# Key and value projections of a cross attention as seven block products each, on one core

## The chip, the cores and the metric

The kernel runs on one core of one Trainium2 chip. The metric is the device time of one execution in microseconds (us). Everything is in float32, and so is every product on the tensor engine. The trace holds two records for each such product (one product of a 128x128 weight block with 512 columns is two records), so a count in the profile is twice the count in the code.

## The reference, cut to what matters

The network has two layers on 32 sequences of 32 positions and width 512: gated attention to a context, self attention, a mixture of 32 experts, and then a second layer, which opens with the cross attention that the change concerns:

```python
q = _split_heads(x1 @ Wq.T + bq, HEADS)        # x1: 32 x 32 x 512
k = _split_heads(x2 @ Wk.T + bk, HEADS)        # x2: 32 x 257 x 512, the context
v = _split_heads(x2 @ Wv.T + bv, HEADS)
scores = jnp.einsum('bhqd,bhkd->bhqk', q, k) / jnp.sqrt(jnp.float32(dh))
attn = jax.nn.softmax(scores, axis=-1)
out = jnp.einsum('bhqk,bhkd->bhqd', attn, v)
```

Each of the 32 sequences has its own 257 context rows, so keys and values are 32 products of 257x512 by 512x512 each. After it come a gated decay attention with group norms, a feed-forward part of width 1024, and one 512x512 product for the spectral mix.

## The kernel before, in words

Rows are worked on in 8 tiles of 128 (four sequences each). After the experts, the last stage runs, tile by tile, three generators on each engine: `head(i)` (layer norm, transposition, queries), `cross(i)` (attention to the context, four context blocks, one for each sequence) and `tail(i)` (everything after it), with `ended(i)` for the spectral mix. A hand-written string, `PLAN_C`, sets the order in which they advance, a piece at a time: c for `cross`, t for `tail`, h for `head`, p for `ended`. Each engine walks the same string, so on each engine the pieces stand in the same order, and the engine does them strictly in that order. Engines wait for each other by counting semaphores.

`cross` has seven pieces for each block, here c0 to c6, and `tail` has fifteen for each tile, t0 to t14. With them the string for a tile is

```
block 0: c0 p t0 | c1 c2 c3 t1 | c4 c5 t2 | c6
block 1: c0 t3 | c1 c2 t4 h0 | c3 c4 t5 h1 | c5 t6 h2 | c6
block 2: c0 t7 | c1 c2 c3 t8 | c4 c5 t9 | c6
block 3: c0 t10 | c1 t11 | c2 c3 t12 | c4 t13 | c5 c6 t14
```

The first tile has `PLAN_F` (no tail; DVE adds expert results and GpSimd issues the gathers for them in its t places), the last `PLAN_Y` (no head).

On the tensor engine (PE) a block before the change is: c0 scores (L1711); c1 and c2 one half of the values each (`values`, L1696, four products of 512 columns); c3 the transposition of the normalised weights (L1726); c4 and c5 the keys of the next block (`keys`, L1679, sixteen products of 257 columns); c6 weights times values (L1752). The scalar engine (ACT) does the exponentials (L890) in c0, copies the transposed weights (L897) in c3, and moves the keys out of PSUM with their bias (`keys_out`, L877) in c4 and c5. The vector engine (DVE) takes maxima and normalises in c0 (L1308 to L1314) and moves the values out with their bias (`values_out`, L1299) in c1 and c2. It does nothing in c4 to c6. GpSimd (POOL) does nothing in `cross`; in the tail it computes the power -1/2 for the norms (L576).

The tail's pieces that matter here: t0 output product (PE) and on DVE layer norm and group sums (L1345 to L1270); t1 a small product of group sums (PE, L1768) and on DVE `group_norm` (L1272, with a power on POOL inside it); t2 transpositions; t3 the qkv product, which ACT squares, copies and scales (L918 to L922); t5 scores of the decay attention, on DVE `decayed` (L1338); t6 its product with the values, which waits for `decayed`; t7 and t8 repeat t0 and t1 in form; t9 two additions on DVE (L1368, L1369); t10 to t13 the feed-forward part; in t13 DVE adds its result and does a layer norm (L1375 to L987). h0 is a layer norm on DVE, h2 the query product.

```python
def values(n, s):
    group(ps[:, bV(n), :],
          [(ctxT_c[:, k, s * S + n * P:s * S + (n + 1) * P], WvT_sb[:, k, :]) for k in range(KD)], v_ps)

def group_norm(w, src, at, bank):
    dve.wait_ge(w.gst_ps, at)
    ...
    TS(gvar, gvar, 0.0, GN_EPS, ALU.max, ALU.add).then_inc(w.gv_rdy, 1)
    ...
    dve.wait_ge(w.grs_rdy, at)
```

The opening of the stage, between the last expert and the first scores, computes keys and values of block 0 and the value row of the 257th context row of all sequences (`lasts`, L1845), while GpSimd gathers the expert results of tile 0 (L650), which DVE adds (`add_experts`, L1259) before the first layer norm.

## Time and profile before

| | us |
|---|---|
| median of 3 runs | 1935.95 (1934.34 to 1938.89) |
| the profiled execution, its own time | 1926.86 |
| its span | 1925.2 |
| PE busy in it | 1844.9 (96%) |
| DVE, ACT, POOL busy | 713.3 (37%), 549.1 (29%), 188.1 (10%) |
| granted TensorE clock, mean | 0.977 of full speed |

The rows are read so: a row of a timeline gives the start in us from the start of the span, the length, the engine, the line of the code, the operation with its operand shapes, and how many instructions are merged in it; in square brackets stands how long the engine had been idle and on whom it had waited. Products overlap: the length of one is longer than the step to the next, so steps are taken from starts. A product group that is written through the helper `group` shows the helper's line, L1416.

### The profile page before, as it was taken

What the parts mean: (1) busy time and instruction counts of PE and PEld (TensorE: products, weight loads), DVE (VectorE), ACT (ScalarE), POOL (GpSimd) and SP (SyncE); (2) the same over time, 40 slices, a digit from 0 to 9 for tenths busy, and PEclk for the clock granted to TensorE, in tenths of its full rate; (3) what the DMA queues carried; (4) which work ended last, traced back from release to release, by engine and by line L of the source; (5) the groups of instructions that cost most, each with busy time, mean ns of one, the idle gap of its engine ahead of it and who ended that gap; (6) DMA issues with size and microseconds to landing.
All of it is one profiled execution on the core that took longest, in us unless ns stands there. A gap on an engine that the chain in (4) does not pass through costs nothing.

```text
span 1925.2 us, 35009 instructions
## 1 busy us (share of the span) xinstructions
PE 1844.9 (96%) x15118; PEld 917.9 (48%) x15118; DVE 713.3 (37%) x1541; ACT 549.1 (29%) x1178; POOL 188.1 (10%) x156
## 2 busy tenths in 40 slices
PE   5999879999999999999989999999999999999977
PEld 2454553333333233223346566665656566565644
DVE  3777753222222222222224443333334333434422
ACT  1444302222222222222222232333323233232321
POOL 2222240000000000000011100001000000100000
PEclk9999879999999999999999999999999999999988
DMA  9754377999999999999962300001000100100000
GB/s 362 236 187 172 141 298 301 402 404 405 404 409 408 408 406 409 409 408 404 366 229 78 121 23 27 14 23 28 23 18 23 29 12 24 28 23 18 12 1 11
DMA packets 84703, 370.67 MB, mean 193 GB/s; under 512 B 7407, under 2 KB 25327, under 8 KB 51841
## 3 DMA queue, kind: packets, MB, share of 16 engines
q1 hardware_dynamic: 79744, 355.78, 48.1%
q0 software_dynamic: 4864, 13.51, 2.0%
q8 instruction: 74, 1.21, 0.3%
q14 instruction: 21, 0.16, 0.0%
HBM read 353.14 MB, written 16.84 MB: 192 GB/s over the span
## 4 chain that ended last, share of the span: by engine, by line
PE 89%; DVE 3%; issue 3%; ACT 3%; DMA 1%; POOL 1%; POOLq 0%; DVEq 0%; ACTq 0%
PE ps L1416 41%; PE ps L1600 17%; PE ps L1612 17%; PE ps L1831 3%; PE ps L1726 1%; PE ps L1480 1%; ACT arena L723 1%; PE ps L1752 1%; PE ps L1588 1%; PE ps L1464 1%; PE ps L1711 1%; PE ps L1426 1%; PE ps L1801 0%; POOL arena L576 0%; PE ps L1809 0%
## 5 line engine op out<-in xcount | busy, mean ns | idle before, releaser
L1416 PE MATMUL ps<-arena 128*128 128x512 f32 (+3 forms) x3120 | 886.3, 440 | 18.4 <-ACT arena L723 6.5
L1416 PEld LDWEIGHTS ps<-arena 128*128 128x128 f32 x3120 | 526.8, 193 | 345.0 <-issue 278.5
L1612 PE MATMUL ps<-arena 128*32 128x512 f32 x2304 | 341.9, 593 | 0.0
L1614 PE MATMUL ps<-arena 128*32 128x512 f32 x768 | 340.9, 593 | 0.0
L1600 PE MATMUL ps<-arena 128*32 128x512 f32 x3072 | 339.5, 596 | 0.2 <-issue 0.2
L576 POOL TENSOR_TENSOR arena<-arena 128x1 f32<-128x1 f32 (+3 forms) x80 | 134.6, 1683 | 974.0 <-DVE arena L982 499.6
L1600 PEld LDWEIGHTS ps<-arena 128*32 128x32 f32 x3072 | 98.1, 108 | 235.2 <-issue 233.7
L1612 PEld LDWEIGHTS ps<-arena 128*32 128x32 f32 x2304 | 92.7, 109 | 215.5 <-issue 212.9
L1218 DVE STREAM_TRANSPOSE arena<-arena 128x512 f32<-128x512 f32 x96 | 68.4, 713 | 215.9 <-ACT arena L831 215.9
L831 ACT ACTIVATE arena<-ps 128x512 f32<-128x512 f32 x96 | 57.3, 597 | 276.4 <-PE ps L1600 276.4
L1228 DVE TENSOR_TENSOR arena<-ps,arena 80x512 f32<-80x512 f32 x32 | 22.0, 688 | 306.8 <-ACT arena L844 306.8
L844 ACT ACTIVATE arena<-ps 32x512 f32<-32x512 f32 x96 | 56.7, 591 | 228.4 <-PE ps L1614 228.4
L880 ACT ACTIVATE arena<-ps,arena 128x257 f32<-128x257 f32 x128 | 60.6, 475 | 186.9 <-PE ps L1416 186.9
L1301 DVE TENSOR_TENSOR arena<-ps,arena 128x512 f32<-128x512 f32 x64 | 44.1, 690 | 124.5 <-PE ps L1416 124.0
L897 ACT ACTIVATE arena<-ps 128x512 f32<-128x512 f32 x64 | 34.8, 595 | 185.3 <-PE ps L1726 185.2
L1308 DVE TENSOR_REDUCE arena<-ps 128x1 f32<-128x257 f32 x128 | 53.5, 418 | 85.8 <-PE ps L1711 85.8
L640 POOL DMA_DIRECT2D y_rows<-arena x32 | 16.6, 517 | 676.7 <-DVE arena L1228 676.7
L1614 PEld LDWEIGHTS ps<-arena 128*32 128x32 f32 x768 | 81.5, 109 | 0.0
L890 ACT ACTIVATE arena<-ps,arena 128x257 f32<-128x257 f32 x128 | 60.5, 475 | 53.4 <-DVE arena L1309 53.3
L1221 DVE TENSOR_TENSOR arena<-arena 128x512 f32<-128x512 f32 x96 | 66.5, 693 | 7.1 <-DVE arena L1218 4.8
L1831 PE MATMUL ps<-arena 128*128 128x512 f32 x128 | 60.9, 621 | 0.0
L838 ACT ACTIVATE arena<-arena 128x512 f32<-128x512 f32 x96 | 53.1, 620 | 0.0
(200 smaller groups left out, 1249.1 us busy)
## 6 DMA issues: line engine op xcount, KB each, us to landing
arena<-in_w SPq DMA_DIRECT2D x64, 4096.0 KB, 18.5
arena<-in_ctxT SPq DMA_DIRECT2D x8, 2056.0 KB, 7.8
arena<-in_ctxT SPq DMA_DIRECT2D x32, 514.0 KB, 3.8
arena<-in_ctx SPq DMA_DIRECT2D x8, 2048.0 KB
xe_rows<-arena SPq DMA_DIRECT2D x8, 640.0 KB, 14.3
y_rows<-arena POOLq DMA_DIRECT2D x32, 160.0 KB, 6.4
arena<-xe_rows SPq DMA_DIRECT2D x30, 160.0 KB, 18.8
arena<-in_wqkv0T SPq DMA_DIRECT2D x1, 3072.0 KB, 19.6
```

Of the source, the lines that this page charges most:

```text
L576: pool.tensor_tensor(dst, src, half_sb[:, 0:src.shape[-1]], ALU.pow).then_inc(done, 1)
L831: act.activation(h_sb[:, t, :].rearrange("p (a c f) -> p a c f", a=HB, c=HB), ps[:, t, :].rearrange("p (a f c) -> p a c f", a=HB, c=HB), A ...
L844: act.activation(yq_sb[s][q4[t], :], ps[q4[3], bQ(s, t), :], ACT.Copy).then_inc(yp_out, 1)
L880: act.activation(kT_c[:, m, :], ps[:, bK(m), 0:S], ACT.Identity, bias=bk_sb[:, m:m + 1], scale=1.0).then_inc(k_ev, 1)
L890: act.activation(P_c[:, g, 0:S], ps[:, bS(g), 0:S], ACT.Exp, bias=nmx[:, g:g + 1], scale=SCALE, accum_out=smc[:, g:g + 1]).then_inc(exp_c, 1)
L1218: dve.transpose(hT[s][:, t].rearrange("p n u -> p (n u)"), h_sb[:, t, :]).then_inc(hT_raw, 1)
L1221: TT(h4, h4, bc(b.rearrange("p c n -> p n c").unsqueeze(3), P, HB, HB, T), ALU.add).then_inc(hb_rdy, 1)
L1416: ins = pe.matmul(dst, lhsT, rhs, start=(n == 0), stop=(n == len(pairs) - 1))
L1600: ins = pe.matmul(ps[q4[n], t, :], xeT[s][:, k, q4[t]], w1_c[:, k, n], start=(k == 0), stop=(k == KD - 1))
L1612: pe.matmul(ps[q4[g], bY(s), :], hT[s][:, g, t, q4[c]], w2_sb[s][:, t * HB + c, :], start=(t == 0 and c == 0), stop=(t == ST - 1 and c == ...
L1614: ins = pe.matmul(ps[q4[ST], bQ(s, t), :], hT[s][:, t, ST, q4[c]], w2_sb[s][:, ST * HB + c, :], start=(c == 0), stop=(c == HB - 1))
L1831: ins = pe.matmul(ps[:, w.b7, :], w.hT2[:, f, :], fw2_sb[:, f, :], start=(f == 0), stop=(f == FT2 - 1))
```

## The change

A block's keys and values (256 of its 257 rows) are computed by the seven-product scheme of Strassen in Winograd's form. The 512x512 weight and the context block are cut into four quarters each; instead of eight block products, seven products of sums of quarters are formed. For the keys a block product is four matrix instructions of 128 columns (`key_product`), for the values two of 256 columns (`value_product`). The sums of weight quarters are formed once, on DVE (`weight_sums`); the four sums of context quarters (T1 to T4) are formed for each block on GpSimd, in c2 and c3 of the block before. The results of the products are combined as they are moved out of PSUM: ACT copies the first product (with the key bias), DVE adds the others, seven additions for the values (c1 to c3) and eight, and a small copy, for the keys (c4 to c6). Three PSUM banks are used in turn, so a product waits until the one that had its bank has been read: the fourth for ACT, the fifth, sixth and seventh for DVE's additions. The keys of the 257th row of all sequences are computed once in the opening (`lasts`), where the values' row was already. The value bias goes in through the accumulation of the weighted values. Keys, values and weights of the first block are set up in the opening, on DVE in a new order. Plans, tails and heads are untouched.

On PE the seven products of the values are spread as v1 to v4 in c1, v5 and half the transpositions in c2, v6, v7 and the other half in c3; the keys as k1 to k4 in c4, k5 and half of the weighted values in c5, k6, k7 and the other half in c6.

```diff
+        NP = 7
+        K_ACT, K_DVE, V_DVE = KH, 9, 7
+        N_T = 4
...
+        kX, kY, kZ = 3, 0, 2
+        vX, vY, vZ = 0, 1, 2
+        def bT(j): return (3, 1)[j]
...
+                    if following:
+                        pool.wait_ge(ctxc_in[(bb + 1) % 2], 16 * ((bb + 1) // 2 + 1))
+                        pool.wait_ge(v_ps, NP * bb + 3)
+                        pool.tensor_tensor(T1, B12, B11, ALU.subtract).then_inc(T_rdy, 1)
+                        pool.wait_ge(T_rdy, N_T * (bb + 1) + 1)
+                        pool.tensor_tensor(T2, B22, T1, ALU.subtract).then_inc(T_rdy, 1)
+                        pool.tensor_tensor(B12, B22, B12, ALU.subtract).then_inc(T_rdy, 1)
+                    yield
+                    if following:
+                        pool.wait_ge(v_ps, NP * bb + 6)
+                        pool.wait_ge(T_rdy, N_T * (bb + 1) + 2)
+                        pool.tensor_tensor(T4, B21, T2, ALU.subtract).then_inc(T_rdy, 1)
+                    yield
...
+            def keys_first(bb):
+                act.wait_ge(k_ps, NP * bb + 1)
+                for m in range(KH):
+                    act.activation(kC11[:, m, :], ps[:, kX, m * P:(m + 1) * P], ACT.Identity,
+                                   bias=bk_sb[:, m:m + 1], scale=1.0).then_inc(k_act, 1)
+
+            def values_first(bb):
+                act.wait_ge(v_ps, NP * bb + 1)
+                act.activation(vC11, ps[:, vX, 0:HF], ACT.Copy).then_inc(v_act, 1)
...
+            def weight_sums(A11, A12, S1, A22, S2, S3, S4):
+                TT(S3, A11, S1, ALU.subtract).then_inc(S_rdy, 1)
+                step(TT(S1, S1, A22, ALU.add))
+                step(TT(S2, S1, A11, ALU.subtract))
+                TT(S4, A12, S2, ALU.subtract).then_inc(S_rdy, 1)
...
+            def keys_first(bb):
+                dve.wait_ge(k_act, K_ACT * bb + KH)
+                dve.wait_ge(k_ps, NP * bb + 2)
+                TT(kC12, half(kY), kC11, ALU.add).then_inc(k_dve, 1)
+                dve.wait_ge(k_ps, NP * bb + 4)
+                TT(kC11, half(kX), kC11, ALU.add).then_inc(k_dve, 1)
+
+            def keys_second(bb):
+                dve.wait_ge(k_ps, NP * bb + 5)
+                dve.wait_ge(k_dve, K_DVE * bb + 1)
+                for m in range(KH):
+                    STT(kC21[:, m, :], ps[:, kY, m * P:(m + 1) * P], dbk[:, m:m + 1], kC12[:, m, :],
+                        ALU.add, ALU.add).then_inc(k_dve, 1)
+                dve.wait_ge(k_dve, K_DVE * bb + 4)
+                TT(kC22, half(kZ), kC21, ALU.add).then_inc(k_dve, 1)
+                TT(kC12, half(kZ), kC12, ALU.add).then_inc(k_dve, 1)
+
+            def keys_third(bb):
+                dve.wait_ge(k_ps, NP * bb + 6)
+                TT(kC21, half(kX), kC21, ALU.add).then_inc(k_dve, 1)
+                dve.tensor_copy(kT_c[:, :, 2 * P:S], klast[:, :, bb:bb + 1]).then_inc(k_dve, 1)
+                dve.wait_ge(k_ps, NP * bb + 7)
+                dve.wait_ge(k_dve, K_DVE * bb + 6)
+                TT(kC12, half(kZ), kC12, ALU.add).then_inc(k_dve, 1)
+
+            def values_first(bb):
+                dve.wait_ge(v_act, bb + 1)
+                dve.wait_ge(v_ps, NP * bb + 2)
+                TT(vC12, ps[:, vY, 0:HF], vC11, ALU.add).then_inc(v_dve, 1)
+                dve.wait_ge(v_ps, NP * bb + 4)
+                TT(vC11, ps[:, vX, 0:HF], vC11, ALU.add).then_inc(v_dve, 1)
+
+            def values_second(bb):
+                dve.wait_ge(v_ps, NP * bb + 5)
+                dve.wait_ge(v_dve, V_DVE * bb + 1)
+                TT(vC21, ps[:, vY, 0:HF], vC12, ALU.add).then_inc(v_dve, 1)
+                dve.wait_ge(v_dve, V_DVE * bb + 3)
+                TT(vC22, ps[:, vZ, 0:HF], vC21, ALU.add).then_inc(v_dve, 1)
+                TT(vC12, ps[:, vZ, 0:HF], vC12, ALU.add).then_inc(v_dve, 1)
+
+            def values_third(bb):
+                dve.wait_ge(v_ps, NP * bb + 6)
+                TT(vC21, ps[:, vX, 0:HF], vC21, ALU.add).then_inc(v_dve, 1)
+                dve.wait_ge(v_ps, NP * bb + 7)
+                dve.wait_ge(v_dve, V_DVE * bb + 5)
+                TT(vC12, ps[:, vZ, 0:HF], vC12, ALU.add).then_inc(v_dve, 1)
...
+            keys_first(0)
+            weight_sums(A11v, A12v, S1v, A22v, S2v, S3v, S4v)
+            keys_second(0)
+            dve.wait_ge(lasts_ps, 2)
...
+            keys_third(0)
+            dve.wait_ge(lasts_ps, 3)
+            dve.tensor_copy(vlast_all[0:B, :], ps[0:B, 7, :]).then_inc(lasts_dve, 1)
+            for stage in (values_first, values_second, values_third):
+                stage(0)
+            step(dve.memset(one.PTd, 0.0))
             dve.wait_ge(gathered0, 32)
             add_experts(0)
...
+            def key_product(bank, Sb, Tb):
+                for m in range(KH):
+                    group(ps[:, bank, chunk(m)], [(Sb[:, k, chunk(m)], Tb[:, k, :]) for k in range(KH)],
+                          k_ps if m == KH - 1 else None)
+
+            def value_product(bank, Tb, Sb):
+                group(ps[:, bank, 0:HF], [(Tb[:, k, :], Sb[:, k, :]) for k in range(KH)], v_ps)
+
+            def keys_first(bb):
+                B11, T3, B21, B22 = keys_of(bb % 2)
+                pe.wait_ge(ctxc_in[bb % 2], 16 * (bb // 2 + 1))
+                if bb > 0:
+                    pe.wait_ge(pt_ev, 2 * (bb - 1) + 1)
+                    if bb % NB == 0:
+                        pe.wait_ge(lastX_rdy, bb // NB)
+                key_product(kX, A11k, B11)
+                if bb > 0:
+                    pe.wait_ge(v_dve, V_DVE * (bb - 1) + 6)
+                pe.wait_ge(T_rdy, N_T * bb + 3)
+                key_product(kY, S2k, T2)
+                if bb > 0:
+                    pe.wait_ge(v_dve, V_DVE * bb)
+                key_product(kZ, S1k, T1)
+                pe.wait_ge(k_act, K_ACT * bb + KH)
+                key_product(kX, A12k, B21)
...
+            def keys_second(bb):
+                B11, T3, B21, B22 = keys_of(bb % 2)
+                pe.wait_ge(k_dve, K_DVE * bb + 1)
+                key_product(kY, S3k, T3)
...
+                B11, T3, B21, B22 = keys_of(bb % 2)
+                pe.wait_ge(T_rdy, N_T * bb + N_T)
+                pe.wait_ge(k_dve, K_DVE * bb + 2)
+                key_product(kX, A22k, T4)
+                pe.wait_ge(k_dve, K_DVE * bb + 6)
+                key_product(kZ, S4k, B22)
...
+            def values_first(bb):
+                B11, T3, B21, B22 = keys_of(bb % 2)
+                if bb > 0:
...
+                value_product(vX, B11, A11v)
...
+                value_product(vY, T2, S2v)
...
+                value_product(vZ, T1, S1v)
+                pe.wait_ge(v_act, bb + 1)
+                value_product(vX, B21, A12v)
+
+            def values_second(bb):
+                B11, T3, B21, B22 = keys_of(bb % 2)
+                pe.wait_ge(v_dve, V_DVE * bb + 1)
+                value_product(vY, T3, S3v)
+
+            def values_third(bb):
+                B11, T3, B21, B22 = keys_of(bb % 2)
+                pe.wait_ge(v_dve, V_DVE * bb + 2)
+                value_product(vX, T4, A22v)
+                pe.wait_ge(v_dve, V_DVE * bb + 5)
+                value_product(vZ, B22, S4v)
...
+                    for half in range(2):
+                        if following:
+                            (keys_second, keys_third)[half](bb + 1)
+                        if half == 0:
+                            pe.wait_ge(pt_ev, 2 * bb + 2)
+                            pe.wait_ge(v_dve, V_DVE * bb + V_DVE)
+                            if b == 0:
+                                pe.wait_ge(vlast_in, 16 * HQ * (i + 1))
+                        for g in range(2 * half, 2 * half + 2):
+                            if g == HG - 1 and following:
+                                pe.wait_ge(k_dve, K_DVE * bb + 2 * K_DVE)
...
+                for m in range(KD):
+                    lo = [(A11k, clastT[:, 0:KH]), (A12k, clastT[:, KH:KD])]
+                    hi = [(S1k, clastT[:, 0:KH]), (A22k, dT)]
+                    group(ps[:, 5, (KD + m) * B:(KD + m + 1) * B],
+                          [(w[:, k, chunk(m % KH)], c[:, k, :]) for w, c in (hi if m >= KH else lo) for k in range(KH)],
+                          lasts_ps if m == KD - 1 else None)
...
+            lasts_turned()
+            keys_first(0)
+            keys_second(0)
+            keys_third(0)
...
+            pe.wait_ge(S_rdy, 4)
             lasts()
+            values_first(0)
+            values_second(0)
+            values_third(0)
```

Where it moves instructions, in three places. First DVE, block 0 of a middle tile, from the group sums of t0 to the next maxima; before (L1268 to L1270 are t0, L1301 the values, L1274 to L1281 `group_norm` in t1):

```order
L1268 TENSOR_TENSOR arena<-arena 128x512
L1269 TENSOR_REDUCE arena<-arena 128x16
L1270 TENSOR_REDUCE arena<-arena 128x16
L1301 TENSOR_TENSOR arena<-ps,arena 128x512 x2
L1274 COPY arena<-ps 128x16
L1275 TENSOR_TENSOR arena<-arena 128x16
L1276 TENSOR_TENSOR arena<-ps,arena 128x16
L1277 TENSOR_SCALAR arena<-arena 128x16
L1278 TENSOR_TENSOR arena<-arena 128x512
L1281 TENSOR_TENSOR arena<-arena 128x512
L1308 TENSOR_REDUCE arena<-ps 128x1
```

and in the changed kernel, from the last value addition (L1384) on (L1412 to L1419 are `group_norm`, L1342 and L1344 the additions of `keys_first`, L1350 to L1354 those of `keys_second`):

```order
L1384 TENSOR_TENSOR arena<-ps,arena 128x256
L1412 COPY arena<-ps 128x16
L1413 TENSOR_TENSOR arena<-arena 128x16
L1414 TENSOR_TENSOR arena<-ps,arena 128x16
L1415 TENSOR_SCALAR arena<-arena 128x16
L1416 TENSOR_TENSOR arena<-arena 128x512
L1419 TENSOR_TENSOR arena<-arena 128x512
L1342 TENSOR_TENSOR arena<-ps,arena 128x2x128
L1344 TENSOR_TENSOR arena<-ps,arena 128x2x128
L1350 SCALAR_TENSOR_TENSOR arena<-ps,arena 128x128 x2
L1353 TENSOR_TENSOR arena<-ps,arena 128x2x128
L1354 TENSOR_TENSOR arena<-ps,arena 128x2x128
```

Where nothing for the keys stood on DVE, their additions now stand behind `group_norm`.

Second PE, the same block, from c0 to the next c0; before (L1711 scores, L1718 bias, L1726 transpositions, L1768 group sums, L1773 transpositions, L1752 weighted values):

```order
L1718 MATMUL ps<-arena 32x512 x4
L1416 MATMUL ps<-arena 128x512 x8
L1726 MATMUL ps<-arena 128x128 x8
L1768 MATMUL ps<-arena 128x32
L1416 MATMUL ps<-arena 128x257 x16
L1773 MATMUL ps<-arena 128x128 x4
L1752 MATMUL ps<-arena 32x32 x32
L1711 MATMUL ps<-arena 32x257 x16
```

and now (L1892 scores, L1900 bias, L1913 transpositions, L1957 group sums, L1962 transpositions, L1939 weighted values; the other rows are products):

```order
L1900 MATMUL ps<-arena 32x128 x16
L1549 MATMUL ps<-arena 128x256 x10
L1913 MATMUL ps<-arena 128x128 x4
L1549 MATMUL ps<-arena 128x256 x4
L1913 MATMUL ps<-arena 128x128 x4
L1957 MATMUL ps<-arena 128x32
L1549 MATMUL ps<-arena 128x128 x20
L1939 MATMUL ps<-arena 32x32 x16
L1962 MATMUL ps<-arena 128x128 x4
L1549 MATMUL ps<-arena 128x128 x8
L1939 MATMUL ps<-arena 32x32 x16
L1892 MATMUL ps<-arena 32x257 x16
```

The values are now fourteen products of 256 columns around the transpositions, the keys twenty-eight of 128 around the weighted values.

Third DVE in the opening, from the last expert result (L1228) to the first layer norm; before:

```order
L1228 TENSOR_TENSOR arena<-ps,arena 80x512
L1248 MEMSET arena 128x2048
L1249 MEMSET arena 128x512
L1250 MEMSET arena 1x128
L1251 TENSOR_REDUCE arena<-arena 16x4
L1254 SCALAR_TENSOR_TENSOR arena<-arena 128x512 x2
L979 BN_STATS arena<-arena 128x6
L981 BN_AGGR arena<-arena 128x2
L982 TENSOR_SCALAR arena<-arena 128x1
L987 TENSOR_SCALAR arena<-arena 128x512
```

and now, from the third step of the first keys (L1358 to L1362) over the values (L1367 to L1384):

```order
L1362 TENSOR_TENSOR arena<-ps,arena 128x2x128
L1397 COPY arena<-ps 32x512
L1367 TENSOR_TENSOR arena<-ps,arena 128x256
L1369 TENSOR_TENSOR arena<-ps,arena 128x256
L1374 TENSOR_TENSOR arena<-ps,arena 128x256
L1376 TENSOR_TENSOR arena<-ps,arena 128x256
L1377 TENSOR_TENSOR arena<-ps,arena 128x256
L1381 TENSOR_TENSOR arena<-ps,arena 128x256
L1384 TENSOR_TENSOR arena<-ps,arena 128x256
L1400 MEMSET arena 128x2048
L1327 SCALAR_TENSOR_TENSOR arena<-arena 128x512 x2
```

The clearing of a large tile (MEMSET of 2048 columns) and all additions of block 0 now stand between the experts and the first addition of gathered rows (SCALAR_TENSOR_TENSOR x2).

## Rows read from the trace of the kernel before

**Rows 1.** Stretches: length, busy us of PE, PEld, DVE, ACT, POOL (instructions), granted clock, DMA, GB/s.

```profile
1000.00:1012.00 12.00, 8.16 (x65) 6.29 (x66) 4.50 (x17) 3.80 (x11) 3.87 (x4) 0.72 0.40 124
...
1250.00:1360.00 110.00, 109.44 (x897) 70.48 (x896) 41.10 (x109) 35.51 (x89) 8.94 (x6) 1.00 0.08 23
```

**Rows 2.** Timeline of PE, opening and one tile: start us, length, what ran.

```profile
975.11 5.25 PE L1416 MATMUL ps<-arena 128*128 128x257 f32 x23
...
1000.57 0.73 PE L1711 MATMUL ps<-arena 32*32 32x257 f32 x32 [1.25 <-DVE arena L1297]
...
1238.90 3.84 PE L1416 MATMUL ps<-arena 128*128 128x128 f32 x32
...
1242.67 0.76 PE L1752 MATMUL ps<-arena 128*32 128x32 f32 x64
...
1254.43 1.03 PE L1726 MATMUL ps<-arena 128*128 128x128 f32 x8
...
1305.08 7.15 PE L1416 MATMUL ps<-arena 128*128 128x512 f32 x16
...
1312.07 1.03 PE L1726 MATMUL ps<-arena 128*128 128x128 f32 x8
...
1312.94 0.31 PE L1768 MATMUL ps<-arena 128*128 128x32 f32 x2
...
1313.08 7.19 PE L1416 MATMUL ps<-arena 128*128 128x257 f32 x32
...
1320.11 0.60 PE L1773 MATMUL ps<-arena 128*128 128x128 f32 x4
...
1320.64 0.76 PE L1752 MATMUL ps<-arena 128*32 128x32 f32 x64
...
1339.59 1.03 PE L1795 MATMUL ps<-arena 128*128 128x128 f32 x8
```

**Rows 3.** Timeline of DVE, same tile and the one before.

```profile
1251.19 0.69 DVE L1301 TENSOR_TENSOR arena<-ps,arena 128x512 f32<-128x512 f32 x1
...
1290.41 0.69 DVE L1375 TENSOR_TENSOR arena<-arena,ps 128x512 f32<-128x512 f32 x1 [8.94 <-PE ps L1831]
...
1292.98 0.55 DVE L987 TENSOR_SCALAR arena<-arena 128x512 f32<-128x512 f32 x1 [0.67 <-POOL arena L576]
...
1309.41 0.68 DVE L1301 TENSOR_TENSOR arena<-ps,arena 128x512 f32<-128x512 f32 x1
...
1312.27 0.69 DVE L1301 TENSOR_TENSOR arena<-ps,arena 128x512 f32<-128x512 f32 x1 [2.18 <-PE ps L1416]
...
1313.29 0.18 DVE L1274 COPY arena<-ps 128x16 f32<-128x16 f32 x1 [0.33 <-PE ps L1768]
...
1317.56 0.69 DVE L1281 TENSOR_TENSOR arena<-arena 128x512 f32<-128x512 f32 x1 [2.87 <-POOL arena L576]
...
1346.05 2.85 DVE L1338 SCALAR_TENSOR_TENSOR arena<-ps,arena 32x512 f32<-32x512 f32 x4 [2.51 <-PE ps L1801]
```

**Rows 4.** Groups by line and shape, DVE and ACT: busy us, mean ns, idle before.

```profile
L1016 DVE TENSOR_TENSOR arena<-arena,ps 128x257 f32<-128x257 f32 x8 | 3.4, 421 | 9.0 <-ACT arena L755 9.0
...
L1309 DVE TENSOR_SCALAR arena<-arena 128x1 f32<-128x1 f32 x128 | 19.6, 153 | 4.4
...
L758 ACT ACTIVATE arena<-ps 128x256 f32<-128x256 f32 x8 | 3.1, 383 | 3.3 <-PE ps L1471 3.3
```

**Rows 5.** Costliest groups of the page: weight loads of the products that go through `group`.

```profile
L1416 PEld LDWEIGHTS ps<-arena 128*128 128x128 f32 x3120 | 526.8, 193 | 345.0 <-issue 278.5
```

**Rows 6.** Timeline of POOL: the power of a group norm.

```profile
1314.17 3.28 POOL L576 TENSOR_TENSOR arena<-arena 128x16 f32<-128x16 f32 x1 [7.43 <-DVE arena L1277]
```

**Rows 7.** Timeline of ACT: the last operation on the qkv projection in block 1.

```profile
1335.19 0.69 ACT L922 ACTIVATE arena<-ps,arena 128x512 f32<-128x512 f32 x1 [0.53 <-POOL arena L576]
```

**Rows 8.** Timeline of DVE, opening of the last stage.

```profile
976.98 1.76 DVE L1248 MEMSET arena<- 128x2048 f32 x1 [0.38 <-issue]
...
990.05 1.54 DVE L1254 SCALAR_TENSOR_TENSOR arena<-arena 128x512 f32<-128x512 f32 x2 [10.32 <-DMA arena<-y_rows,uidx]
```

More of the change, by code:

```diff
@@ L128, in perceiver_kernel @@
         M_sb = keep.take(KD, D)
[L129 removed]
+        id_sb, ones_sb, gones_sb = (keep.take(P) for _ in range(3))
+        wts = keep.take(2, NT)
+        early = keep.at
+        tri_sb = keep.take(P)
         causal_sb, iotad_sb = keep.take(T), keep.take(E)
```

283 lines of the change are left out of this document (153 added, 130 removed).

## The prediction

> **What bounds the kernel now.** I read the stretches first. In the middle of the last stage PE is busy 109.44 of 110 us at a granted clock of 1.00, DVE 41.10, ACT 35.51, POOL 8.94 [rows 1]: PE's instruction stream is the time, and whatever PE does less comes off it, provided no wait takes its place. Before the change there are nearly no such waits, because what other engines do for PE has a whole piece of slack. So the question is not how much DVE has to do but when, and for that I read the timelines of one tile, engine by engine.
>
> Steps on PE from starts [rows 2]: values, 16 records of 512 columns, from 1305.08 to 1312.07, 6.99 us; keys, 32 records of 257 columns, from 1313.08 to 1320.11, 7.03 us, so 0.22 a record; 32 records of 128 columns from 1238.90 to 1242.67, 0.118 a record. DVE starts on a PSUM result 0.20 after PE's last record has had its step (1312.07 [rows 2], 1312.27 [rows 3]). An addition of 257 columns with one operand in PSUM takes 0.42 [rows 4]; I use that for 256, and 0.29, halfway to the 0.153 of one column [rows 4], for 128.
>
> **Products.** A block of seven products has 28 records of 256 columns for the values (6.16 us) and 56 of 128 for the keys (6.61), 12.77 against 14.02: 1.25 us less a block. A value product (v1 to v7) is 0.88, a key product (k1 to k7) 0.94. There are 31 blocks beside the opening: 39 us, if nothing waited.
>
> The 128-column step is the number to doubt, since each record brings its own weight load, of 0.193 us in the mean [rows 5]; the 32 records above have one load each too, and step at 0.118 [rows 2], so the load runs beside the product before it. I take 0.118. The Trainium skill, TensorE: Matmul & The Clock Gate, section Back-to-back issue gap, says instead that in a stream of loads and products both set the spacing: 81 ns at 128 columns against 131 ns at 512. By that ratio, an estimate, the keys of a block would take 15 us; the row of 0.118 does not bear that out here.
>
> **Evictions.** DVE had two additions of 0.69 a block in c1 and c2. It now has seven of 0.42 there and, for the keys, six of 0.42, two of 0.29 and a small copy: 6.2 us against 1.4. Some 19 us more a tile fit into its idle time. But PE now waits for them product by product, and they stand in DVE's queue behind the tail's and head's work, which the order of DVE shows. I lay one tile out.
>
> Waits in every block: after k7 the last addition (0.20 + 0.42) covers only one quarter of the weighted values (0.76 / 4 [rows 2]): 0.43, four times, 1.7. v7 needs three additions after v5 (0.20 + 3 x 0.42 = 1.46); PE has half the transpositions (0.87 / 2) and v6 in between, 1.32: 0.15 in blocks 0, 2 and 3 (in block 1 a t piece lies between), 0.45.
>
> Block 0. v5 waits for DVE's first addition, which stands behind t0's norm and group sums: DVE is free at 1309.41 [rows 3], so it is done at 1309.83; PE is there at 1305.08 + 4 x 0.88 = 1308.60. 1.25. Then k5 waits for the first key addition, which stands behind `group_norm`: that ended 5.31 after the start of the small product it needs (1312.94 [rows 2] to 1317.56 + 0.69 [rows 3]), of which 3.28 are the power on POOL [rows 6]. With the addition 5.73; PE needs 0.14 for the small product and 3.76 for k1 to k4. 1.85.
>
> Block 1. Values started at 1339.59 - 6.99 = 1332.60 [rows 2], the third product would be done at 1335.24, but ACT is with the qkv product until 1335.19 + 0.69 [rows 7], and its copy of 256 columns takes 0.38 [rows 4]: v4 waits 1.0. Then k2 waits for the sixth value addition, behind t4's addition and h0's layer norm: 3.1 as for the like sequence from 1290.41 to 1292.98 + 0.55 [rows 3]. v5 ends at 1336.26 + 2 x 0.88 = 1338.02; DVE is through at 1338.02 + 1.46 + 3.1 + 0.42 = 1343.0, PE arrives at 1338.02 + 2 x 0.43 + 0.87 (t4) + 2 x 0.88 + 0.94 = 1342.45: 0.55. t6 waits for `decayed`, 2.85 [rows 3] plus 0.20; between t5 and t6 PE now has h1 (0.53, as from 1320.11 to 1320.64 [rows 2]), k5 and half the weighted values (0.38), 1.85, where it had 3.5 us of keys: 1.2.
>
> Block 2. As block 0: v5 0.65 (DVE free at 1251.19 [rows 3], first product at 1254.43 - 6.99 [rows 2]), k5 1.85; and the two additions of t9, of 0.69 each, come between the key additions, so the last wait is 0.6 longer.
>
> Block 3. k7 waits for `keys_second` (2 x 0.29 + 2 x 0.42 = 1.4), which stands behind t13's addition and layer norm (1290.41 to 1293.53 [rows 3], 3.1): 4.7 with the 0.20, against k5, half the weighted values and k6, 2.26. 2.45.
>
> Sum of waits in a tile 13.55; products 4 x 1.25 = 5.0 less: **8.55 us longer a tile**. Tiles 1 to 6: 51. The last tile, without heads and with three sets of keys, has waits of 10.6 and saves 4.6: 6.
>
> The first tile has no tail, but DVE's additions of expert rows and POOL's gathers take the t places, the latter ahead of the context sums. Its bounds are all its savings and only the waits of every block (-3) and a whole tile's waits (+14 less 5, plus some 5 for the gathers); I take 7, nearer to the upper end, since the same queueing occurs.
>
> **Context sums on POOL.** No row shows a subtraction there. Below, DVE's 0.42 bounds it; above, the power, 3.28 for 16 columns [rows 6], at 0.2 a column 52 us. I take 1.0, near the lower end, because a subtraction needs no series. They have cover: T1 to T3 may start after v3 and are due at k2, after v4 to v7, the transpositions and k1, 5.3 us and about 0.9 of waits; T4 has more. So they cost nothing up to 2 us apiece.
>
> **Opening.** PE starts at 975.11 [rows 2]. It now does 0.4 of transpositions, 6.6 of keys with about 3 of waiting in them (four weight sums of 0.69 stand on DVE between the first and second key additions), the last rows' keys (32 records of 32 columns, at most 0.118: 3.8), the last rows' values 3.5 and the values 6.2: 998.6. DVE's last addition is done at 999.2, the clearing (1.76 [rows 8]), which had stood in idle time, at 1001.0. Then the gathered rows are added, which began at 990.05 [rows 8] and led to the first scores at 1000.57 [rows 2]: **11 us later**. Bounds 5 (short records much cheaper, weight sums earlier) and 16 (PE at the lower clock after waiting). Loads, the bias through PSUM (as many PE columns) and the other weight sums (under the last expert) cost nothing.
>
> **Sum.** 51 + 6 + 7 + 11 = 75 on 1926.9, the profiled execution: 2002. That execution lies 9 us under the median of 1936, so I forecast **2011** for the median. With each unknown at its lower end (5 a tile, 3, -3, 5) 1971, at its upper (12, 9, 14, 16) 2047.
>
> **Rivals.**
> (a) The other side: the cover holds, and the saving is kept. DVE would stay below 60% busy, which speaks for it; the order on DVE speaks against. It decides at k5: if `group_norm` and the first addition were done within 3.9 us of the small product rather than 5.73, and likewise at the other places, only the waits of every block stayed (2.15 a tile): 6 x 2.85 and 3 in the last tile saved, 2 in the first, 5 lost in the opening: -17, 1919. Chance 0.08.
> (b) POOL's subtraction is slow. From 2 us on PE waits at k2; at 4 us for 5.8 a block, 31 times, 180 more than no cover lost: about 2190. Only the power speaks for it. Chance 0.06.
> (c) The waits let the clock fall. In the 12 us after 1000, with waits of PE, the granted clock was 0.72, between the levels of 1.2 and 2.4 GHz [rows 1], 3.4 us lost. Twice a tile in seven tiles that is 47: 2058. Against it: PE's waits here are 2.5 us at most, with full work between. Chance 0.12.
> (d) Weight loads bound the short products: a key record then takes 0.193 [rows 5], 56 of them 4.2 us more a block, 31 times, 130: 2141. The row of 0.118 speaks against it. Chance 0.02. The page named above would have it so.
>
> **Numbers.** The forecast has 0.72. Faster by over 0.2% (about what a measurement of this kernel can tell from no change) is (a), 0.08; within 0.2% lies only the gap between (a) and the low forecast, 0.02; slower 0.90. The range runs from the lower end of the terms, a little widened, to (c): 1965 to 2065; (a), (b) and (d), 0.16, are left out.
>
> **What would show it.** In the profile after: key products at 0.118 a record and value products at 0.22; PE idle before products some 13 us a tile, released by DVE additions at v5, k5 and k7 and by ACT at v4, longest (near 2 us) before k5 in blocks 0 and 2 and k7 in block 3; a tile longer by 8 to 9 us; first scores near 1012; POOL operations of about 1 us. I am wrong if PE shows no waits at k5, if its records are longer than these steps, or if POOL releases it.

## The result, and the profile after

The changed kernel takes **2039.72 us** (median, 2032.35 to 2044.19) where the kernel before took 1937.42 beside it: 1.0525 times as long, 95% interval 1.0489 to 1.0561. The profiled execution took 2041.04, its span is 2039.4, 114.2 more than before.

The page: busy time by engine, and the granted clock in the 40 slices.

```profile
PE 1861.5 (91%) x16502; PEld 1034.2 (51%) x16502; DVE 865.9 (42%) x2003; ACT 523.7 (26%) x1146; POOL 275.1 (13%) x280
...
PEclk8999879999999999999888999999999999999988
```

PE was 96% busy and is now 91%: gaps came in. Its busy time rose by 16.6 us all the same (from 1844.9), though the products are shorter (products_alone below); stretches at the lower clock, also below, are in it. First scores of each tile, from the timelines of PE, show where:

| stretch | before | after | longer | forecast |
|---|---|---|---|---|
| start to first scores | 1000.57 | 1024.83 | 24.3 | 11 |
| first tile | 74.62 | 88.70 | 14.1 | 7 |
| tiles 1 to 6 | 108.99, then 112.08 or 112.09 | 120.34, then 123.21 to 124.09 | 69.0 | 51 |
| last tile to the end | 180.6 | 187.4 | 6.9 | 6 |

What PE waited for, whole execution: line that waited, what ended it, us in all, times, longest.

```profile
PE ps L1549 <- DVE arena L1342: 24.3, 14, 1.7
PE ps L1721 <- DMA arena<-xe_rows: 17.0, 1, 17.0
PE ps L1549 <- DVE arena L1354: 16.6, 8, 2.7
PE ps L1559 <- DVE arena L1035: 11.4, 3, 7.1
PE ps L1549 <- DVE arena L1367: 10.3, 15, 1.2
PE ps L1939 <- DVE arena L1362: 10.3, 27, 0.9
...
PE ps L1998 <- DVE arena L1475: 8.1, 7, 1.5
PE ps L1549 <- DVE arena L1381: 7.3, 7, 2.9
...
PE ps L1549 <- ACT arena L931: 5.2, 7, 0.7
...
PE ps L1549 <- POOL arena L702: 0.3, 1, 0.3
```

L1549 is a product. Released by L1342 it is k5, by L1354 k7, by L1367 v5, by L1381 k2, by L931 (ACT) v4; L1939 are the weighted values behind the last key addition, L1998 is t6. POOL, with all its context sums, released PE once.

PE in block 0 of a middle tile (the place of [rows 2]): values, transpositions, group sums, k1 to k4, k5.

```profile
1366.78 3.73 PE L1549 MATMUL ps<-arena 128*128 128x256 f32 x16
1371.56 1.13 PE L1549 MATMUL ps<-arena 128*128 128x256 f32 x4 [1.05 <-DVE arena L1367]
...
1375.40 0.31 PE L1957 MATMUL ps<-arena 128*128 128x32 f32 x2
1375.55 3.82 PE L1549 MATMUL ps<-arena 128*128 128x128 f32 x32
1381.10 1.16 PE L1549 MATMUL ps<-arena 128*128 128x128 f32 x8 [1.73 <-DVE arena L1342]
```

DVE and POOL over the same time: `group_norm`, then the first key additions.

```profile
1376.46 0.68 DVE L1416 TENSOR_TENSOR arena<-arena 128x512 f32<-128x512 f32 x1
1380.02 0.69 DVE L1419 TENSOR_TENSOR arena<-arena 128x512 f32<-128x512 f32 x1 [2.87 <-POOL arena L602]
1380.63 0.42 DVE L1342 TENSOR_TENSOR arena<-ps,arena 128x256 f32<-128x256 f32 x1
```

```profile
1376.63 3.28 POOL L602 TENSOR_TENSOR arena<-arena 128x16 f32<-128x16 f32 x1 [1.88 <-DVE arena L1415]
```

DVE idles 2.87 us for the power of [rows 6], while k2 is done and its addition stands one place further back. PE stops 1.73 us for it.

PE at the end of block 3, and the stretches around it (length, busy us of PE, PEld, DVE, ACT, POOL, granted clock, DMA share, GB/s):

```profile
1348.48 1.16 PE L1549 MATMUL ps<-arena 128*128 128x128 f32 x8
1351.79 1.50 PE L1549 MATMUL ps<-arena 128*128 128x128 f32 x8 [2.15 <-DVE arena L1354]
1353.21 1.03 PE L1939 MATMUL ps<-arena 128*32 128x32 f32 x32
1354.17 1.93 PE L1950 MATMUL ps<-arena 16*32 16x128 f32 x32
```

```profile
990.00:1000.00 10.00, 10.00 (x44) 8.05 (x43) 1.12 (x4) 0.00 (x0) 0.97 (x1) 0.53 0.54 169
1016.40:1025.00 8.60, 6.58 (x52) 5.99 (x68) 1.15 (x3) 1.88 (x2) 1.89 (x3) 0.71 0.00 0
1056.15:1062.00 5.85, 5.84 (x27) 5.85 (x28) 1.02 (x3) 0.00 (x0) 0.00 (x0) 0.50 0.01 2
1349.60:1353.60 4.00, 1.85 (x25) 1.51 (x24) 2.51 (x8) 0.00 (x0) 0.25 (x1) 0.86 0.00 0
1353.60:1358.00 4.40, 4.26 (x89) 2.66 (x84) 0.74 (x2) 1.39 (x3) 0.00 (x0) 0.50 0.00 0
```

Behind the wait for k7 the granted clock is 0.50 of full speed, the lower of the two levels: the products of the last rows (L1950) take 1.93 us, against 1.08 at the upper level in k7_fill below. Steps from k7 to the first products of the next tile lose some 3 us so. The same happens in the opening (990 to 1000) and in the first tile.

### The profile page after: what moved, and what is told of

It reads as the page before. It is cut to its first block, busy times and chain, and to the rows that moved or that the text cites. A ratio compares the mean times of both kernels' runs of the same rounds, so it can differ in the third digit from the quotient of the medians.

```text
span 2039.4 us, 38643 instructions
## 1 busy us (share of the span) xinstructions
PE 1861.5 (91%) x16502; PEld 1034.2 (51%) x16502; DVE 865.9 (42%) x2003; ACT 523.7 (26%) x1146; POOL 275.1 (13%) x280
## 4 chain that ended last, share of the span: by engine, by line
PE 74%; DVE 10%; issue 8%; POOL 5%; ACT 2%; DMA 1%; DVEq 0%; POOLq 0%; ACTq 0%
PE ps L1549 28%; PE ps L1733 16%; PE ps L1745 16%; POOL arena L602 3%; PE ps L2020 3%; PE ps L1613 1%; PE ps L1892 1%; ACT arena L938 1%; PE ps L1913 1%; PE ps L1939 1%; PE ps L1962 1%; DVE arena L1475 1%; PE ps L1721 1%; PE ps L1950 1%; DVE arena L1027 1%
## 5 line engine op out<-in xcount | busy, mean ns | idle before, releaser
L1549 PE MATMUL ps<-arena 128*128 128x128 f32 (+4 forms) x4312 | 891.2, 361 | 83.0 <-DVE arena L1342 24.3
L1549 PEld LDWEIGHTS ps<-arena 128*128 128x128 f32 (+1 forms) x4312 | 628.4, 196 | 321.5 <-issue 178.2
L666 POOL DMA_DIRECT2D y_rows<-arena x32 | 16.6, 517 | 677.7 <-DVE arena L1276 677.7
L938 ACT ACTIVATE arena<-ps,arena 128x257 f32<-128x257 f32 x128 | 60.6, 475 | 115.4 <-DVE arena L1440 115.3
L699 POOL TENSOR_TENSOR arena<-arena 128x256 f32<-128x256 f32 x31 | 22.6, 728 | 245.8 <-PE ps L1549 245.8
L769 ACT ACTIVATE arena<-ps,arena 128x128 f32<-128x128 f32 x64 | 24.1, 457 | 99.2 <-PE ps L1962 99.2
```

The costliest lines, as they stand in the source:

```text
L938: act.activation(P_c[:, g, 0:S], ps[:, bS(g), 0:S], ACT.Exp, bias=nmx[:, g:g + 1], scale=SCALE, accum_out=smc[:, g:g + 1]).then_inc(exp_c, 1)
L1549: ins = pe.matmul(dst, lhsT, rhs, start=(n == 0), stop=(n == len(pairs) - 1))
```

## The experiments

The theory: the products are as short as forecast; what is lost are waits on DVE's (and once ACT's) queue order, and the clock that falls behind some of them. The rivals: short records are slower than their steps; DVE or its memory access is simply full, so that a wait removed turns up elsewhere.

The kernel before was timed beside each experiment, with medians from 1931.31 to 1937.55 (1937.42 beside the change). So ratios and plain differences of a whole time disagree by some us, and a gain is better read from the tiles. Tiles 2 to 6 are called middle tiles here; tile 1 is some 2 to 5 us shorter in every run.

**k5: additions inside `group_norm` (norm_split).** DVE only, cut to the place where the additions now stand:

```diff
                 step(TT(w.t1.rearrange(...), ..., ALU.subtract))
+                if ahead:
+                    keys_first(ahead.pop())
                 dve.wait_ge(w.grs_rdy, at)
```

> On DVE alone the two first key additions of the next block go into group_norm, between its subtraction and the wait for POOL's power, instead of behind it; nothing else moves. Theory (PE waits because the additions stand behind other work in DVE's queue): the waits before k5, 24.3 us in all, fall under 4 us; the power's 3.28 us then cover the additions, group_norm ends at most 0.4 us later than now, and the kernel is 16 to 24 us shorter, 2016 to 2024. Rival (DVE and POOL are short of capacity or of a shared port, so that any order pays): the waits turn up at k6, at the next transpositions or at the last key addition, and less than 6 us is gained.

2011.42 us, 1.0411 (1.0372 to 1.0451) times the kernel before, so 1.1% off the change's ratio, 22 us (28 between the medians). The waits at k5 are gone, middle tiles are 119.5 to 120.2, and tiles 1 to 6 are 21.9 shorter together. Not a new wait but the power's own time took the additions in:

```profile
1365.81 0.68 DVE L1418 TENSOR_TENSOR arena<-arena 128x512 f32<-128x512 f32 x1
1367.06 0.42 DVE L1342 TENSOR_TENSOR arena<-ps,arena 128x256 f32<-128x256 f32 x1 [0.57 <-PE ps L1558]
1368.74 0.42 DVE L1344 TENSOR_TENSOR arena<-ps,arena 128x256 f32<-128x256 f32 x1 [1.26 <-PE ps L1558]
1369.30 0.69 DVE L1423 TENSOR_TENSOR arena<-arena 128x512 f32<-128x512 f32 x1
```

Queue order, then, and not capacity.

**The clock: two experiments at k7.** First `keys_second` ahead of the layer norm's last step (k7_ahead, cut), which shortens the wait; then products that nobody reads in the wait (k7_fill), which only keep PE at work.

```diff
-                layer_norm(1, xt, w.xn, 2 * m + (w.base + 1), w.xn_rdy, w=w)
+                moments(1, xt, w)
+                if second:
+                    keys_second(second.pop())
+                normed(1, xt, w.xn, 2 * m + (w.base + 1), w.xn_rdy, w=w)
```

> On DVE alone keys_second goes into the layer norm behind t13 in block 3, ahead of its normalisation, while POOL has the root; nothing else moves. The wait before k7 should fall from 2.15 us to between 0.8 and 1.3. Theory (the clock falls because of that wait): with the shorter wait the 4.4 us of half clock behind it go too, and a tile is 4 us shorter, the kernel some 25 to 30, 2010 to 2015. Rival (the clock falls there for another reason, or falls on the shorter wait as well): only the wait's own 0.9 to 1.3 us a tile, 6 to 9 us in all, 2030 to 2034.

```diff
                 key_product(kX, A22k, T4)
+                if bb > 0 and bb % NB == 0:
+                    for _ in range(2):
+                        pe.matmul(ps[:, 1, :], WoT_sb[:, 0, 0:P], WoT_sb[:, 0, :], start=True, stop=True)
                 pe.wait_ge(k_dve, K_DVE * bb + 6)
```

> Two products of 512 columns (4 records, 1.75 us), whose results nobody reads, are put on PE into the wait before k7 of block 3, seven times in all; k7 still starts when its addition is done, so no wait is really shortened. Theory (an idle PE lets the clock fall): the visible wait is 0.4 us, the granted clock stays at 1.00 behind it, and each of the seven places gives back some 3 us: 18 to 22 us shorter, about 2019. Rival (the clock falls for another reason): half clock behind k7 as now, the time within 3 us of 2040.

k7_ahead: 2020.55 (1.0462, 1.0433 to 1.0491), some 12 us by the ratio and 19 between the medians, between the two expected numbers; tiles 1 to 6 are 19.9 shorter together, 3.3 each where the theory had 4. The wait is 0.95 (1.03 the first time). Of its seven places the clock still falls at three, and at four it stays at 1.00. One of each:

```profile
1346.00:1352.00 6.00, 4.79 (x96) 3.60 (x108) 3.18 (x9) 0.60 (x2) 0.56 (x1) 0.81 0.00 0
1708.16:1714.16 6.00, 4.75 (x113) 3.41 (x113) 3.49 (x11) 1.51 (x3) 0.56 (x1) 1.00 0.01 3
```

k7_fill: 2024.53 (1.0492, 1.0461 to 1.0524), some 6 us by the ratio, 15 between the medians, and 13.4 in tiles 1 to 6 together, where 18 to 22 were expected. At the place itself the theory holds:

```profile
1344.92 1.88 PE L1850 MATMUL ps<-arena 128*128 128x512 f32 x4
1347.23 1.16 PE L1549 MATMUL ps<-arena 128*128 128x128 f32 x8 [0.43 <-DVE arena L1354]
...
1349.17 1.08 PE L1953 MATMUL ps<-arena 16*32 16x128 f32 x32
```

```profile
1345.00:1351.00 6.00, 5.31 (x97) 3.36 (x111) 3.25 (x9) 0.68 (x2) 0.29 (x1) 1.00 0.01 3
```

but only every second middle tile is 120.43 long; the others are 122.1 to 122.4, because there the clock now falls behind k5 in block 0 (in the tile from 1228.68: 0.65 from 1254.0 to 1258.2), after the same wait of 1.74 that leaves it at 1.00 a tile later. The fall had moved to the next wait.

**All three (orders_fill):** norm_split, k7_ahead, and one such product.

> Three edits together: the first key additions inside group_norm, keys_second inside the layer norm behind t13, and one product of 512 columns (0.87 us) that nobody reads in what is left of the wait before k7. If the gains add, a tile loses 3.5 at k5, 1.2 at k7 and 3.1 of half clock: 115.4 us, 1978 in all. If the fall of the clock moves to another wait, as it did in every second tile with the products in the wait alone: 116.5 to 118, 1985 to 1998. If neither adds: 2010.

1990.36 us (1.0291, 1.0250 to 1.0331). Every middle tile is 115.62 to 115.64, within 0.3 of the first of the three numbers, and the clock stays up through six tiles:

```profile
1112.00:1811.00 699.00, 664.76 (x6560) 503.73 (x6560) 371.90 (x1019) 192.47 (x511) 121.17 (x132) 1.00 0.09 27
```

With k5's wait out of the way the clock falls nowhere else in these tiles. The whole is 12 us over the expected 1978: in the profile the first tile gained nothing (88.71), and the first scores stand at 1031.66, 6.8 us later than in the change. The wait for the expert rows (below) was a long one, but so was the change's.

**Products without their additions (products_alone).** DVE's stages are not called from the second block on, and PE's waits on `k_dve` and `v_dve` stand under `if bb == 0`.

> From the second block on, DVE's additions for keys and values and the last key's copy are left out, and PE's waits for them with them; ACT's copies of k1 and v1 and POOL's context sums stay, so scores and weighted sums are made of old keys and values. It shows what the products are worth with no wait in them. Theory (the products are shorter as predicted, 1.25 us a block, and all that is lost is waits and clock): a tile of 107 to 109.5 us (112.08 less 5.0, the waits of 0.74 for ACT and 1.1 for the decayed scores left), granted clock 1.00, the whole 1915 to 1935 since the opening stays long. Rival (records of 128 and 256 columns, one weight load each, are slower than 0.118 and 0.22): a tile of 112 us or more without any wait, the whole 1945 and more.

1932.01 us (0.9990, 0.9961 to 1.0019); middle tiles of 108.57 to 108.59 (the last 108.93) at clock 1.00. PE's own time in one, without the 1.84 us of waits left, is 106.74; before, 112.08 less 0.51 is 111.57. The products save **4.83 us a tile, forecast 5.0**: the rival of slow short records is out. Even so the whole is no faster, since the opening and the first tile give back what is left: in the profile the first scores come 26.1 us later than before, 7.2 of that in the wait for the expert rows (below), and the first tile is 2.7 longer.

**Context sums on DVE instead of POOL (sums_on_dve).** `context_sums(bb + 1)` behind `values_second`, `context_last(bb + 1)` behind `values_third`, POOL's pieces empty.

> The context sums (T1 to T4 of every block) go from POOL to DVE, behind values_second and values_third; four additions of 0.42 us, 1.7 a block. Theory (DVE's queue is what PE waits for, POOL's sums cost nothing): DVE is later at the last value additions, at group_norm and at the first key addition, 0.5 to 1.5 us a block, 15 to 45 us longer, about 2070, with more waits at k5 and v7. Rival (POOL's operations slow DVE's by as much as they take off it): within 8 us of 2040.

2056.39 us (1.0657, 1.0623 to 1.0692), 16.7 over the change between the medians, at the low end of what was expected; the rival is out. Middle tiles are 125.2 to 125.7, 0.6 us a block more at most, the most of it at k2 (11.6 in all, from 7.3) and k5 (27.5, from 24.3). GpSimd earns its part: in the change the four sums take 0.68 to 0.76 us each on it and cost PE 0.3 us in all. In products_alone, where the other waits are gone, PE waits for them twice in the first tile, 4.9 us in all.

```profile
L702 POOL TENSOR_TENSOR arena<-arena 128x256 f32<-128x256 f32 x31 | 23.6, 763 | 0.0
L699 POOL TENSOR_TENSOR arena<-arena 128x256 f32<-128x256 f32 x31 | 22.6, 728 | 245.8 <-PE ps L1549 245.8
```

**The opening (opening).** DVE only, cut (the clearing goes from its old place):

```diff
-            dve.wait_ge(wV_in, 16 * WV)
             keys_first(0)
-            weight_sums(A11v, A12v, S1v, A22v, S2v, S3v, S4v)
             keys_second(0)
+            dve.wait_ge(wV_in, 16 * WV)
+            weight_sums(A11v, A12v, S1v, A22v, S2v, S3v, S4v)
+            step(dve.memset(one.PTd, 0.0))
```

> On DVE alone, in the opening, the four weight sums of the values go behind keys_second, and the clearing of PTd behind them, into DVE's 7.6 us of idle time. Theory: PE's wait of 2.69 us ahead of k7 goes, the clearing's 2.1 us ahead of the first layer norm go, and without that wait the clock does not fall to 0.53 for ten us, 4 to 5 us more: first scores some 9 to 10 us earlier against PE's last expert product than the 44 us now, 2030 in all. Rival (the clock falls anyway, since keys and additions alternate there): only 4.8 us, 2035.

2039.20 us (1.0555, 1.0532 to 1.0579): nothing gained, a miss for both. From PE's transposition of the last rows to the first scores it is 43.07 us instead of 44.25. PE's wait ahead of k7 shrank from 2.69 to 0.60, but 1.66 came back as a wait for the late weight sums; the clearing's 2.3 us went; and the lower clock was only spread otherwise, 0.71 and 0.78 in the two halves of the keys and values where it had been 0.53 and 0.95, and 0.60 in the ten us before the first scores.

**Only the values by seven products (values_only).** Keys as before the change; POOL forms T3 once the keys are done.

```diff
+            def keys_out(bb, first):
+                for m in range(first, first + 2):
+                    act.wait_ge(k_ps, KD * bb + (m + 1))
+                    act.activation(kT_c[:, m, :], ps[:, bK(m), 0:S], ACT.Identity,
+                                   bias=bk_sb[:, m:m + 1], scale=1.0).then_inc(k_act, 1)
...
+                    if following:
+                        pool.wait_ge(k_ps, KD * (bb + 2))
+                        pool.tensor_tensor(B12, B22, B12, ALU.subtract).then_inc(T_rdy, 1)
```

> Values by seven products as in the change, keys in full products of 257 columns with ACT's eviction as before the change; POOL makes the third context sum once the keys are done. Theory (the keys' chain of additions is what costs most): of the waits those at v5 (1.05 and 0.26) and v4 (0.74) stay, 2.05 a tile and 0.2 each for PE running empty, against 4 x 0.83 saved, so a tile of 111 to 112.5 us, no fall of the clock, and with an opening 3 to 6 us longer 1922 to 1940, no change against the kernel before. Rival (any eviction by chained additions gives back more than the products save): a tile over 114, 1955 and more.

1943.58 us (1.0055, 1.0029 to 1.0082), a little over the range; middle tiles 112.57 or 112.58, 0.1 over the range for them. So with the values alone a tile loses 0.5 us, with the keys too 11.1 to 12.0: the keys' products save least (0.42 us a block), and their additions stand behind the most.

**Towards a better version.** In values_ordered the orders on ACT and DVE are changed at v4 and v5:

```diff
+                if ahead:
+                    values_first(ahead.pop())
                 act.activation(w.v1, ps[:, w.b5, :], ACT.Copy)
...
+                if ahead:
+                    bb = ahead.pop()
+                    values_first(bb)
+                    values_second(bb)
                 dve.reduce_sum(w.gs[:, H:2 * H], w.t1.rearrange("p (g c) -> p g c", g=H), AX.X).then_inc(w.gs_rdy, 1)
```

> The kernel with seven products for the values alone, and two orders changed. On ACT the copy of v1 in block 1 goes between the squares and the copy of the qkv product, instead of behind all of them. On DVE the first five value additions go into the group sums ahead of their last reduction, in blocks 0 and 2. Theory (the waits are a matter of the queues' order): v4's wait of 0.74 and v5's of 1.05 and 0.35 go, with 0.2 each for PE running empty, 2.7 us a tile: 109.8 to 110.3 where 112.58 stands, 1922 to 1928, faster than the kernel before. Rival (they turn up again at v7, at the small product of the group sums or at the tail's transpositions): 111.5 to 112.5 a tile, 1936 to 1943.

1931.23 us (1.0011, 0.9991 to 1.0030): tiles of 110.66, 1.9 gained and 1.4 under the kernel before, a little less than expected (0.46 stays at v5), and the whole even with the kernel before, where 1922 to 1928 was expected. values_late takes the first block out of the scheme (cut):

```diff
+            for n in range(2):
+                pe.wait_ge(k_act, n + 1)
+                for k in range(KD):
+                    ins = pe.matmul(ps[:, bK(n), :], ctxT_c[:, k, n * P:(n + 1) * P], WvT_sb[:, k, :],
+                                    start=(k == 0), stop=(k == KD - 1))
+                ins.then_inc(v_ps, 3 + n)
             lasts()
...
-        def bK(m): return (3, 0, 2, 1)[m]
+        def bK(m): return (0, 2, 3, 1)[m]
```

> The kernel before this, with the first block's values and the last rows' values in full products (so the opening is as it was before the change), the weight sums behind the first softmax, the keys' groups in another order of banks, and in the first tile DVE's additions of expert rows two pieces later. Theory (what the tiles gain, 1.42 us each, was given back in the opening, some 6 us, and in the first tile, 3): first scores 25 to 26 us after the experts' last product, a first tile of 75 to 76.5, tiles of 110.7 as before this edit; 1920 to 1925, 0.4 to 0.6% faster than the kernel before the change. Rival (the first tile pays for the late weight sums, or the gain lies in the spread of the start): 1928 to 1932, no difference.

1932.17 us (0.9984, 0.9963 to 1.0006), no difference and a miss, though not by the rival's cause. Opening 27.7 and first tile 74.46, nearly as expected, but tiles of 112.46: with the other order of banks the first key group waits up to 1.7 us, six times, for a value addition behind the head's layer norm. values_banks takes that part back:

> As the kernel before this, but the keys' four groups in the banks 3, 0, 2, 1 again, so that the first group waits for the first transposition's eviction and no longer for the sixth value addition, which stands behind the head's layer norm in block 1. Theory: the six waits of 1.7 us there go, a tile is 110.7 where it was 112.46, first tile and opening stay (75 and 28 us): 1920 to 1925, 0.3 to 0.7% faster than the kernel before the change. Rival (the time is set at the start of the experts, by the wait for the gathered rows): 1928 to 1934.

**1926.08 us, 0.9955 (0.9933 to 0.9976)**: tiles of 110.66 or 110.67, opening 27.2, first tile 76.52. It is 0.45% under the kernel before, little but clear of the interval, and over 5% under the change. PE in the middle of it ([rows 1] has 109.44 busy, with POOL at 8.94):

```profile
1250.00:1360.00 110.00, 108.96 (x961) 79.76 (x951) 49.07 (x132) 37.00 (x92) 19.77 (x22) 1.00 0.08 23
```

**The start of the experts (before_again).**

> The kernel before the change, once more, for PE's wait for the gathered expert rows, 9.1 us in its profile and 17.0 in that of the change; kernels with the same instructions there have had 7.9 to 19.7. If the change made the wait longer, it is 9 to 10 here again; if its size is a matter of how the transfers happen to meet, anything from 8 to 18.

9.7 us. Over all fourteen profiles the longest wait there is 7.6 to 10.7 (eight of them, with both of the kernel before) or 15.0 to 17.0 (six, with the change's own), and kernels with the same instructions there have either. It goes with how long SP needs to issue two loads of expert weights, 33.4 to 34.0 in the former, 30.3 to 30.4 in the latter; of the change and of norm_split:

```profile
250.31 30.33 SPq L504 DMA_DIRECT2D arena<-in_w  x2
```

```profile
250.96 33.43 SPq L504 DMA_DIRECT2D arena<-in_w  x2
```

That is the first wait alone. Later experts can wait as well: 0.2 to 0.9 us, thirteen times, in values_late and values_banks. All of PE's waits for expert rows, of the kernel before and of values_banks (us in all, times, longest):

```profile
PE ps L1588 <- DMA arena<-xe_rows: 9.1, 1, 9.1
```

```profile
PE ps L1687 <- DMA arena<-xe_rows: 19.2, 14, 10.7
```

Counted so, five profiles have 7.9 to 9.7 us and nine have 16.3 to 19.7, and values_ordered, values_late and values_banks are among the long ones although SP took 33.6 to 34.0 in them. So some 8 us of any single execution hang on these waits, and SP's issue does not account for all of them; the profiled execution of values_banks (1932.65) is among the longest of its twelve. Whether the change's earlier load of the last context rows, issued right behind these two, makes the long case possible is open. Both profiles of the kernel before are short, too few to tell, and nearly all of its other executions lie between 1925 and 1945 us, so long cases may be among them. It wasn't tried apart.

## Why the prediction was right, and where it was short

**The bound and the products.** PE's stream bounds, and it became shorter by what the steps said: 4.83 us a tile (forecast 5.0). k1 to k4 step at 0.112 a record (3.57 us from 1340.10 to 1343.67 for 32), against 0.118 assumed. Rival (d) is out by that. The Trainium skill (TensorE: Matmul & The Clock Gate, Back-to-back issue gap), by which loads and products both set the spacing, is not borne out by this trace: 56 key records at 0.112 make 6.3 us a block, not the 15 that the prediction worked out from it.

**The waits of a tile**, forecast against the tile from 1357.08: v5 1.25 and 1.05, k5 1.85 and 1.73, v4 1.0 and 0.74, k2 0.55 and 0.68, t6 1.2 and 1.10, in block 2 v5 0.65 and 0.26 and k5 1.85 and 1.73, k7 2.45 and 2.15. The last key addition was too dear (0.43 four times and 0.6, measured 0.26 twice and 0.66), and v7 never waited. In all 13.55 forecast, 10.62 idle in the trace. Each of the 11 stops also costs the 0.2 to 0.3 us in which PE runs empty: its own time is 112.59, 5.85 over products_alone; less 3 for the clock that is 2.8. Idle and that together, 13.4, is near the forecast sum, in part by luck: terms that were too large (v7 and the last key addition most) made up for what the stops cost beside their idle time. By the prediction's own figures 1.25, 1.85 and 2.45 should read 1.23, 1.83 and 2.44, which moves the sum by less than 0.1.

**What failed: the clock.** The step "Against it: PE's waits here are 2.5 us at most, with full work between" put rival (c) at 0.12 and left its price out of the sum. It is part of the main case: not twice a tile but once, behind k7, some 3 us (priced at 3.4 from [rows 1]). That is the tile's missing 3, 18 us over tiles 1 to 6. k7_fill shows at the place that it hangs on PE being idle, orders_fill that the tile is 7.6 us shorter without k5's wait, most of k7's and the fall. What decides which stops are followed by a fall stays open: in k7_ahead the same 0.95 has it at some places and not at others.

**First tile and opening.** 14.1 against 7, at the upper bound: waits of 16.1 us where there were 7.5, and more of the lower clock, of which 5.85 us behind k2's wait of 2.93 is one piece. The first tile in the change, then before:

```profile
1024.83:1113.53 88.70, 72.42 (x822) 62.35 (x826) 49.64 (x135) 17.43 (x52) 22.88 (x27) 0.88 0.21 60
```

```profile
1000.57:1075.19 74.62, 67.11 (x665) 46.93 (x669) 32.62 (x85) 21.16 (x57) 14.40 (x15) 0.95 0.27 80
```

In the opening 24.3 against 11. Of it 5.5 arose at the experts' start, which the prediction put at nothing ("Loads ... cost nothing") and which is the two-sized wait above. From the transposition of the last rows on it is 44.25, before (from the first keys, 975.11) 25.46: 18.8, where the bound was 16 with "PE at the lower clock after waiting". That was the mechanism, and its size was short: ten us at 0.53 lose some 4.7 and 8.6 us at 0.71 some 2.5 (estimates from the two rows above), nearly all of the 7.8 beyond the forecast. No run kept the clock up there, so this share is read from rows and not shown by an experiment.

**Context sums.** 0.68 to 0.76 us for 1.0, free as argued; (b) is out. The prediction's sign of being wrong "if POOL releases it" came up once, for 0.3 us. (a) is out: the cover did not hold at k5, 1.73 late.

**The sum.** 75 forecast, 114.2 measured: opening 13.3 short, first tile 7.1, tiles 18, last tile 0.9. Sign, places (but for v7) and order of the waits were right; the clock was mis-sized in each of the first three. Between the medians it is 102 instead of 114, since the profiled execution of the kernel before, with the short wait for expert rows, lies 9 to 11 us under its median. The median came 29 us over the forecast of 2011, and 18 us under (c)'s 2058. It is still under the sum's own upper end of 2047, but only just, with the tiles at 11.5 longer of the 12 allowed, the first tile at its bound and the opening beyond it. So the range held by its width, with a cost inside it that the sum had left out.

## What to carry to other kernels

Fewer products pay on a full PE only if what they are chained to is done in time, so lay out the queue of the engine that evicts, not its busy share: DVE was 42% busy, and one addition behind a wait for GpSimd cost 1.73 us where its block saved some 1.2. Put such additions inside the wait, and take the scheme only where the saving is large against the additions: here for the values, not the keys. And count a stop of PE twice, as idle time and as the half clock that may follow. Whether more than three PSUM banks in turn would take the waits off was not tried.

## What the runs showed of the hardware that was not expected

- The clock's fall is no fixed price of a wait: behind k7's 2.15 us it was 0.50 for over 4 us; behind k7's 0.95 in k7_ahead there was a fall at some places (0.81 over 6 us) and none at others; behind k5's 1.73 there was none in the middle tiles of the change, and behind the same 1.74 in every second tile once another stop had been filled.
- Four records whose results nobody reads, put into a stop of PE, kept the clock at 1.00 there and did not delay k7.
- PE's waits for expert rows come to 7.9 to 9.7 us or to 16.3 to 19.7, some 8 us apart, also in kernels with the same instructions there. The first wait goes with SP's issue of two loads (30.3 us, or 33.4 and more), the later ones do not.
